# Five keep-busy products fewer, and the first maxima, a value's copy and the weight pieces moved, in the prologue of a gated cross-attention block

## The chip, the cores and the metric

One core of one Trainium2 chip runs the whole kernel. The metric is the time of one execution on the device in microseconds (us). The engines are PE (TensorE), DVE (VectorE), ACT (ScalarE), POOL (GpSimd) and SP (SyncE, which here issues DMAs and nothing else). Each runs its own stream of instructions in order, and they wait for each other by semaphores.

## The reference

The block takes x (4 x 512 x 512) and a context (4 x 1024 x 512), all float32. It has 16 heads of 32 columns.

```python
def qdq(x):                      # int8 fake quantisation along the last axis
    s = max(max(abs(x)) / 127, 1e-8)
    return clip(round(x / s), -127, 127) * s

def xattn(x, cond):
    q = qdq(x) @ qdq(wq).T + bq
    k, v = split(cond @ wkv.T + bkv)
    o = softmax(q k.T / sqrt(32)) @ v          # per head
    return qdq(o) @ qdq(wp).T + bp

def ffn(x):                      # gate_w, up_w, down_w rounded to float8_e4m3
    return ((silu(x @ gate_w * gate_scale) * (x @ up_w * up_scale)) @ down_w) * down_scale

x = x + tanh(g_xattn) * xattn(layernorm(x), ctx)
x = x + tanh(g_ffn) * ffn(layernorm(x))
```

## The kernel before

The four batches are computed one after the other. For each, a first stage makes q, k and v, a second the scores, exponentials and weighted sums in 32 units (4 groups of 4 heads by 8 tiles of 128 keys), and a third the projection and the feed-forward part. For batches 1 to 3 the first stage lies inside the stages of the batch before. For batch 0 it is a prologue of some 70 us, and only the prologue and the 32 units behind it are touched by the change.

**Products in two halves.** Keys and values are made from float16 pairs: a high part and a low part (what the high part left). A tile of keys (`K0` to `K7`) or values (`V0` to `V7`) takes 12 products of 128 x 512 into one bank of PSUM. The bias of a value tile is a 13th product, of ones with `bv_rows`, that POOL prepares (lines 735 to 743, semaphore `bv_set`). The 8 x 512 columns of values are copied out by ACT (line 909, semaphore `v_out`), the highs of q and k are made by ACT (lines 843, 850), the lows by DVE (`q_low` line 1178, `k_low` line 1165).

**The order on PE in the prologue** (lines 1777 to 1842): the keys; 12 products whose result nobody reads (line 1796); the turn of the quantised wq (line 1536), behind DVE's clip of it (line 1271); the first 8 of the 13 products of V0 and V1 (line 1570); the turn of quantised x (line 1536, behind ACT's line 876); its scales (line 1593); the four q tiles (line 1552, behind ACT's copies, line 880); the last 5 products of V0 and of V1 (lines 1576, 1577, behind `bv_set`); then V2 to V7 (line 1552); then the scores of the first unit (line 1716). `A_BANK` gives each result its bank. V0, V2 and V6 share bank 1; V1, V3 and V7 share bank 2, so that V2 waits until ACT has copied V0, and V3 until it has copied V1.

**The steps of the maxima.** The shift that each softmax needs is a maximum over keys. It is made in steps, laid into the products by tables. A step D (`difference`) is two products of q with half the difference of two halves of the keys (line 1621), which ACT turns into a doubled Relu (line 896, semaphore `diff_kept`). A step R is two products of q with the second half of the keys into banks 6 and 7 (line 1688), which DVE adds to the Relu and reduces to a maximum (line 1211, two instructions and a read of the accumulator each). PE's next R waits for DVE's reduction of the one before (`m_free`). A step S turns a finished group's maxima on PE (line 1643), and DVE clips them into `crow` (line 1198). `rest(n)` is the pair R of step n and D of step n+1. `STEPS0` says behind which tile's half each pair goes: before, `Q3` carries D0, `V2` to `V5` two pairs each (R0 to R7), `V6` S of group 0 and R8, `V7` R9; the rest goes to the units (`UNIT_STEPS0`).

**The weight pieces.** The gate, up and down weights arrive as 36 pieces of 256 KB and are rounded to float8 on the way. For each piece SP loads it (line 564), DVE makes its magnitude in two instructions (`w_magnitudes`, lines 1301 and 1304), and POOL rounds it in two (`round_weights`, lines 722 and 724, semaphore `w_done`). There are four buffers: pieces 0 to 3 are loaded early, and the load of piece k waits until piece k-4 is rounded. Before, DVE makes one magnitude behind each of V2 to V7.

**SP's queue.** SP issues in the order in which its program is written:

```python
stack(kst, (khi, khi, klo), 1)
load_weights(W_AHEAD["shift0"])     # up to piece 7: waits for w_done of pieces 1, 2, 3
shift_row(0, 0)                     # crow of group 0 into row 96 of qst
```

`shift_row` is line 588. The first scores of unit 0 (line 1716) contract 97 rows, of which row 96 is this one, and wait for the DMA to land (`stack_in[0]`).

Of the kernel before, what the change touches and what calls it, by code (L numbers as in the profile page):

```python
# [22 lines left out]
CT, NT, MT, FT = C // P, N // P, M // P, F // P  # L23
# [28 lines left out]
BEGUN = 2  # L52
# [20 lines left out]
def rest(n):  # L73

    return [("R",) + DIFFS[n][1:]] + DIFFS[n + 1:n + 2]


STEPS0 = {"Q3": [DIFFS[:1]], "V2": [rest(0), rest(1)], "V3": [rest(2), rest(3)], "V4": [rest(4), rest(5)],
          "V5": [rest(6), rest(7)], "V6": [[("S", 0, 0)], rest(8)], "V7": [rest(9), []]}
_first = 10  # L80

UNIT_STEPS0 = {u: rest(_first + u) if _first + u < len(DIFFS) else [] for u in range(G * MT)}
# [136 lines left out]
def a_count(name):  # L219
    return A_SEQ0.index(name) + 1  # L220


def by_act(name):

    return name[0] == "V"
# [117 lines left out]
def build(nc, ctxT, x, wq, wkvT, wp, gate_w, up_w, down_w, bqT, bkT, bv, bp, gsT, usT, ds,  # L343
          g_x, g_f, out):
    with ExitStack() as ctx:
# [135 lines left out]
        def bank(n, rows=P, dt=F32):  # L481
            v = ps[0:rows, n, :]
            return v if dt == F32 else v.bitcast(dt)
# [330 lines left out]
        def _(act):  # L814
# [72 lines left out]
            def differences(b, steps):  # L887

                for s in steps:
                    if s[0] != "D":  # L890
                        continue
                    n, first_bank = DIFFS.index(s), diff_bank(b, s)
                    act.wait_ge(diff_full, diff_count(b, s))
                    if n >= 2:
                        act.wait_ge(m_free, FREE_AFTER[b, ("R",) + DIFFS[n - 2][1:]])
                    nc.scalar.activation(kept(b, n), ps[:, first_bank:first_bank + 2, :], ACT.Relu,  # L896
                                         scale=2.0).then_inc(diff_kept, 1)

            for c in range(CT):
                if c == CT - 1:  # L900
                    for part in STEPS0[f"Q{c}"]:
                        differences(0, part)
                q_half(0, c)
            for name in A_SEQ0[-MT:]:
                for part in STEPS0.get(name, []):
                    differences(0, part)
                if by_act(name):
                    act.wait_ge(a_full, a_count(name))
                    nc.scalar.copy(vv[:, int(name[1:]), :], bank(A_BANK[name])).then_inc(v_out, 1)  # L909
            def projection_weights(u):  # L910

                if u in WP_ROWS:
# [122 lines left out]
        def _(dve):  # L1035
# [150 lines left out]
            def maxima(b, steps):  # L1186

                for s in steps:
                    kind, g, i = s
                    if kind in "WD":  # L1190
                        continue
                    if kind == "K":
                        if b == 0 or g > 0:
                            key_difference(b, g)
                        continue
                    if kind == "S" and b == 0:
                        dve.wait_ge(m_full, FULL_AT[b, s])
                        nc.vector.tensor_scalar(crow_rows(g), bank(PAIR, HG), CMAX, -CMAX, ALU.min,
                                                ALU.max).then_inc(crow_ready, 1)
                        continue  # L1200
                    if kind == "S":
                        dve.wait_ge(d_full, d_full_count(b - 1, f"TOP{g}"))
                        nc.vector.tensor_scalar(crow_rows(g), bank(d_bank(b - 1, f"TOP{g}"), HG), CMAX, -CMAX, ALU.min,
                                                ALU.max).then_inc(d_free, 1)
                        continue
                    n = g * PARTS + i
                    dve.wait_ge(m_full, FULL_AT[b, s])
                    dve.wait_ge(diff_kept, b * len(DIFFS) + n + 1)
                    for k in range(2):
                        j = 2 * (i % 2) + k  # L1210
                        ins = nc.vector.tensor_tensor_reduce(  # L1211
                            kept(b, n)[:, k, :], bank(PAIR + k), kept(b, n)[:, k, :], 1.0, -3.0e38, ALU.add,
                            ALU.max, mx[:, g % 2, i // 2, 0, j:j + 1])
                    ins.then_inc(m_free, 1)
# [109 lines left out]
            for n in range(CT):  # L1324
# [5 lines left out]
                    first_lows(K_SEQ0[7:])  # L1330
                if 1 <= n < CT - 1:
                    q_low(0, n - 1, a_free)
            for n in range(MT):
                if n == BEGUN + 1:
                    key_difference(0, 1)
                for k, part in enumerate(STEPS0.get(f"V{n}", [])):
                    maxima(0, part)
                    if n == BEGUN:
                        q_low(0, CT - 2 + k, a_free)
                if n >= MT - W_EARLY:  # L1340
                    w_magnitudes()

            for b in range(B):
# [187 lines left out]
        def _(pe):  # L1531
# [256 lines left out]
            for k, name in enumerate(K_SEQ0):  # L1788
# [3 lines left out]
                    pe.wait_ge(dve_setup, 3 * CT)  # L1792
                a_wait(name)
                k_product(bank(A_BANK[name]), int(name[1:]), a_full)
            for _ in range(CT * 3):
                nc.tensor.matmul(bank(6), wkv_hi[:, 0, 0:P], ctx_hi[:, 0, 0:512], start=True, stop=True)
            pe.wait_ge(pool_setup, 7)
            pe.wait_ge(wq_clipped, 1)
# [31 lines left out]
            pe.wait_ge(bv_set, 5)  # L1830
            for n in range(BEGUN):
                end_v(bank(A_BANK[f"V{n}"]), n, a_full, (ones[:, :], bv_rows[:, :]))
            for n in range(BEGUN, MT):
                first_v(n)
            pe.wait_ge(rows_set, 1 + G)
# [163 lines left out]
```

## Time and profile before

| | us |
|---|---|
| median of 3 runs | 893.6 (893.58 to 894.18) |
| profiled execution | 892.01, span 890.2 |
| PE busy | 855.0 (96%) |
| DVE busy | 674.1 (76%) |
| ACT busy | 563.1 (63%) |
| POOL busy | 256.3 (29%) |

The span runs from the first to the last instruction of the profiled execution; 1.8 us of that execution's time lie around it. Busy time is the sum of an engine's instructions with overlaps taken once. The granted clock of TensorE is 1.00 of full speed over the whole run by the profile's own account. Lines such as L1716 are lines of the kernel before.

### The profile page before, as it was taken

The numbers are of one execution on the slowest core, as the hardware profiler recorded it, in microseconds if no ns is written. First come the engines' busy times: TensorE is split into PE (matmuls) and PEld (weight loads), VectorE is DVE, ScalarE is ACT, GpSimd is POOL, SyncE is SP. The second block draws the span as 40 slices with busy tenths as digits, with TensorE's granted clock in tenths as the row PEclk, the third lists the DMA queues.
The fourth block names the chain that finished last, engine by engine and source line by source line (L and its number), as shares of the span: only waits on it lengthen the run. The fifth ranks groups of instructions, "written<-read, shape, count | busy, mean of one in ns | idle before, by whom it ended". The sixth has DMA issues, their size and how long they took to land.

```text
span 890.2 us, 14133 instructions
## 1 busy us (share of the span) xinstructions
PE 855.0 (96%) x5188; PEld 334.5 (38%) x5188; DVE 674.1 (76%) x1307; ACT 563.1 (63%) x771; POOL 256.3 (29%) x254
## 2 busy tenths in 40 slices
PE   7989999999899999899999999999999999999998
PEld 3432222354333322235433332225433322224984
DVE  5978967979766778878876768986967778779322
ACT  5758987752466569783555649885356779972440
POOL 1337767872257300020017700002002210011340
PEclk9999999999999999999999999999999999999999
DMA  9335334221111332200211143300010024200001
GB/s 322 124 92 151 89 112 112 83 83 44 47 46 39 101 108 60 48 1 1 48 30 48 38 120 91 76 5 1 15 39 1 1 52 113 57 1 25 14 1 48
DMA packets 37317, 55.32 MB, mean 62 GB/s; under 512 B 9024, under 2 KB 15488, under 8 KB 37248
## 3 DMA queue, kind: packets, MB, share of 16 engines
q1 hardware_dynamic: 35328, 48.13, 19.0%
q0 software_dynamic: 1920, 6.29, 2.4%
q8 instruction: 41, 0.67, 0.3%
q14 instruction: 28, 0.23, 0.1%
HBM read 31.21 MB, written 4.19 MB: 40 GB/s over the span
## 4 chain that ended last, share of the span: by engine, by line
PE 74%; DVE 11%; ACT 7%; issue 6%; DMA 0%; SPq 0%; ACTq 0%; DVEq 0%
PE ps L1552 37%; PE ps L1753 8%; PE ps L1716 8%; PE ps L1733 8%; ACT r L946 5%; PE ps L1688 4%; DVE acc L1236 4%; PE ps L1747 3%; PE ps L1536 2%; PE ps L1784 1%; PE ps L1761 1%; DVE kst L1211 1%; PE ps L1643 1%; DVE r L1211 0%; DVE q_reg L1178 0%
## 5 line engine op out<-in xcount | busy, mean ns | idle before, releaser
L946 ACT ACTIVATE r<-ps 128x1024 f32<-128x1024 f32 (+1 forms) x300 | 253.3, 902 | 54.2 <-PE ps L1716 51.7
L1211 DVE CUSTOM_DVE_ANT_0 kst<-ps,kst 128x512 f32<-128x512 f32 x192 | 124.5, 685 | 30.3 <-PE ps L1688 29.0
L1716 PE MATMUL ps<-qst,kst 97*128 97x512 f16 x512 | 137.1, 382 | 3.5 <-DVE acc L1316 1.8
L1733 PE MATMUL ps<-r,vv 128*32 128x512 f32 x1024 | 136.4, 604 | 3.4 <-ACT r L946 3.2
L1236 DVE TENSOR_TENSOR acc<-acc,r 128x1024 f32<-128x1024 f32 x120 | 138.7, 1216 | 0.0
L896 ACT ACTIVATE kst<-ps 128x1024 f32<-128x1024 f32 x96 | 98.1, 1022 | 54.2 <-PE ps L1621 53.9
L1552 PE MATMUL ps<-xs,w_up 128*128 128x512 f16 (+1 forms) x480 | 93.3, 337 | 0.0
L1552 PE MATMUL ps<-xs,w_gate 128*128 128x512 f16 (+1 forms) x480 | 93.2, 337 | 0.0
L1716 PEld LDWEIGHTS ps<-qst,kst 97*128 97x128 f16 x512 | 40.4, 97 | 139.3 <-ACT r L946 89.4
L1021 ACT ACTIVATE qst<-ps,gs_c 128x512 f32<-128x512 f32 (+1 forms) x60 | 36.1, 601 | 67.1 <-PE ps L1552 67.1
L1496 DVE SCALAR_TENSOR_TENSOR xq<-ps,us_c,qst 128x512 f32<-128x512 f32 (+1 forms) x60 | 38.6, 643 | 45.5 <-PE ps L1552 45.5
L1552 PEld LDWEIGHTS ps<-xs,w_gate 128*128 128x128 f16 x480 | 45.1, 98 | 36.2 <-issue 5.2
L1552 PEld LDWEIGHTS ps<-xs,w_up 128*128 128x128 f16 x480 | 44.0, 98 | 35.8 <-issue 8.2
L1688 PE MATMUL ps<-k_reg,q_reg 32*128 32x512 f16 x256 | 49.6, 385 | 3.7 <-DVE mx L1211 3.0
L1621 PE MATMUL ps<-acc,q_reg 32*128 32x512 f16 x256 | 49.6, 384 | 3.1 <-issue 3.1
L750 POOL TENSOR_TENSOR xres<-xres,bp_bc 128x512 f32<-128x512 f32 x12 | 14.9, 1268 | 129.6 <-ACT r L954 129.1
L711 POOL TENSOR_TENSOR rstd<-mv,mhalf 128x4 f32<-128x4 f32 (+1 forms) x9 | 10.3, 1145 | 144.4 <-DVE mv L1098 127.5
L1236 DVE TENSOR_TENSOR acc<-r 128x1024 f32<-128x1024 f32 x24 | 28.3, 1221 | 28.9 <-ACT r L946 28.9
L1552 PE MATMUL ps<-wkv_hi,ctx_hi 128*128 128x512 f16 x120 | 45.6, 380 | 1.1 <-ACT vv L909 1.1
L1747 PE MATMUL ps<-r,esel 128*32 128x512 f32 x352 | 46.4, 599 | 0.0
L1552 PE MATMUL ps<-wkv_hi,ctx_lo 128*128 128x512 f16 x120 | 45.5, 379 | 0.0
L1552 PE MATMUL ps<-wkv_lo,ctx_hi 128*128 128x512 f16 x120 | 45.5, 379 | 0.0
(204 smaller groups left out, 1399.0 us busy)
## 6 DMA issues: line engine op xcount, KB each, us to landing
kst<-k_reg SPq DMA_DIRECT2D x192, 64.0 KB
qst<-q_reg SPq DMA_DIRECT2D x192, 32.0 KB
xs<-in_x SPq DMA_DIRECT2D x4, 1024.0 KB, 6.9
cf<-in_ctxT POOLq DMA_DIRECT2D x16, 256.0 KB, 3.4
xres<-in_x SPq DMA_DIRECT2D x3, 1024.0 KB, 5.2
out<-xres SPq DMA_DIRECT2D x12, 256.0 KB, 2.0
acc<-in_down_w SPq DMA_DIRECT2D x10, 256.0 KB, 2.7
acc<-in_ctxT POOLq DMA_DIRECT2D x8, 256.0 KB, 3.3
```

What stands on the lines that cost most here:

```text
L896: nc.scalar.activation(kept(b, n), ps[:, first_bank:first_bank + 2, :], ACT.Relu, scale=2.0).then_inc(diff_kept, 1)
L946: nc.scalar.activation(prob[:, s:s + heads, :], ps[:, first_bank:first_bank + heads, :], ACT.Exp, scale=SCALE).then_inc(exp_done, 1)
L1211: ins = nc.vector.tensor_tensor_reduce(kept(b, n)[:, k, :], bank(PAIR + k), kept(b, n)[:, k, :], 1.0, -3.0e38, ALU.add, ALU.max, mx[:, g % ...
L1236: nc.vector.tensor_tensor(sums, other, prob[:, p:p + ADD_HEADS, :], ALU.add).then_inc(p_dve, 1)
L1496: nc.vector.scalar_tensor_tensor(out=fus[:, i % 2, width], in0=bank(d_bank(b, name))[:, width], scalar=us_c[:, tile:tile + 1], in1=tmp[:, ...
L1552: mm = nc.tensor.matmul(out, l, r, start=(k == 0), stop=(k == len(terms) - 1))
L1621: mm = nc.tensor.matmul(bank(first_bank + k), qhi[rows, g, i // 2 * P:(i // 2 + 1) * P], kdiff[rows, g % 2, :], start=True, stop=True)
L1688: mm = nc.tensor.matmul(bank(PAIR + k), qhi[rows, g, t * P:(t + 1) * P], khi[rows, g, 512:1024], start=True, stop=True)
L1716: mm = nc.tensor.matmul(bank(first_bank + k), kst[0:97, g % 2, j + k, t * P:(t + 1) * P], qst[0:97, g % 2, j + k, :], start=True, stop=True)
L1733: mm = nc.tensor.matmul(ps[j * DH:(j + 1) * DH, O_BANK, :], vv[:, t, h * DH:(h + 1) * DH], prob[:, p_slot(b, u, j), :], start=(t == 0), st ...
L1747: mm = nc.tensor.matmul(ps[j * DH:(j + 1) * DH, DEN_BANK, :], esel[:, g, :], prob[:, p_slot(b, u, j), :], start=(u == (MT - 1 if b else 0) ...
L1753: mm = nc.tensor.matmul(out[:, cols], f2_at(b, part, i)[:, t * P:(t + 1) * P], w_down[:, i, cols], start=(i == 0 and part == 0), stop=(i = ...
```

## The change

The change rewrites parts of the prologue of batch 0.

- PE issues 7 products at line 1796 where there were 12.
- The steps of the maxima begin one tile earlier: R0 and D1 go between the end of V1 and V2; V2, V3 and V4 carry the pairs of R1 to R6; V5 carries R7 alone. V6 (S, R8) and V7 (R9) and all units stay as they are.
- ACT does the Relu of D0 ahead of the third query half where it was ahead of the fourth, and copies V0 ahead of the fourth where it was behind it.
- DVE makes the low part of Q2 ahead of R0, that of Q3 and the key difference of group 1 behind R0 and ahead of R1. (Before, these stood behind R0, behind R1 and ahead of R2.)
- DVE makes no weight magnitude behind V2, one each behind V3 to V6, and two behind V7.

SP's program and POOL's are not touched.

```diff
--- before.py
+++ after.py
@@ -75,8 +75,8 @@
     return [("R",) + DIFFS[n][1:]] + DIFFS[n + 1:n + 2]
 
 
-STEPS0 = {"Q3": [DIFFS[:1]], "V2": [rest(0), rest(1)], "V3": [rest(2), rest(3)], "V4": [rest(4), rest(5)],
-          "V5": [rest(6), rest(7)], "V6": [[("S", 0, 0)], rest(8)], "V7": [rest(9), []]}
+STEPS0 = {"Q3": [DIFFS[:1]], "V1": [rest(0)], "V2": [rest(1), rest(2)], "V3": [rest(3), rest(4)],
+          "V4": [rest(5), rest(6)], "V5": [rest(7), []], "V6": [[("S", 0, 0)], rest(8)], "V7": [rest(9), []]}
 _first = 10
 
 UNIT_STEPS0 = {u: rest(_first + u) if _first + u < len(DIFFS) else [] for u in range(G * MT)}
@@ -896,17 +896,21 @@
                     nc.scalar.activation(kept(b, n), ps[:, first_bank:first_bank + 2, :], ACT.Relu,
                                          scale=2.0).then_inc(diff_kept, 1)
 
+            def first_values(name):
+                act.wait_ge(a_full, a_count(name))
+                nc.scalar.copy(vv[:, int(name[1:]), :], bank(A_BANK[name])).then_inc(v_out, 1)
+
             for c in range(CT):
+                if c == 2:
+                    for part in STEPS0[f"Q{CT - 1}"]:
+                        differences(0, part)
                 if c == CT - 1:
-                    for part in STEPS0[f"Q{c}"]:
-                        differences(0, part)
+                    first_values("V0")
                 q_half(0, c)
-            for name in A_SEQ0[-MT:]:
+            for name in A_SEQ0[-MT + 1:]:
                 for part in STEPS0.get(name, []):
                     differences(0, part)
-                if by_act(name):
-                    act.wait_ge(a_full, a_count(name))
-                    nc.scalar.copy(vv[:, int(name[1:]), :], bank(A_BANK[name])).then_inc(v_out, 1)
+                first_values(name)
             def projection_weights(u):
 
                 if u in WP_ROWS:
@@ -1330,14 +1334,14 @@
                     first_lows(K_SEQ0[7:])
                 if 1 <= n < CT - 1:
                     q_low(0, n - 1, a_free)
-            for n in range(MT):
-                if n == BEGUN + 1:
+            q_low(0, CT - 2, a_free)
+            for n in range(1, MT):
+                for part in STEPS0[f"V{n}"]:
+                    maxima(0, part)
+                if n == 1:
+                    q_low(0, CT - 1, a_free)
                     key_difference(0, 1)
-                for k, part in enumerate(STEPS0.get(f"V{n}", [])):
-                    maxima(0, part)
-                    if n == BEGUN:
-                        q_low(0, CT - 2 + k, a_free)
-                if n >= MT - W_EARLY:
+                for _ in range((0, 0, 0, 1, 1, 1, 1, 2)[n]):
                     w_magnitudes()
 
             for b in range(B):
@@ -1792,7 +1796,7 @@
                     pe.wait_ge(dve_setup, 3 * CT)
                 a_wait(name)
                 k_product(bank(A_BANK[name]), int(name[1:]), a_full)
-            for _ in range(CT * 3):
+            for _ in range(7):
                 nc.tensor.matmul(bank(6), wkv_hi[:, 0, 0:P], ctx_hi[:, 0, 0:512], start=True, stop=True)
             pe.wait_ge(pool_setup, 7)
             pe.wait_ge(wq_clipped, 1)
@@ -1830,6 +1834,9 @@
             pe.wait_ge(bv_set, 5)
             for n in range(BEGUN):
                 end_v(bank(A_BANK[f"V{n}"]), n, a_full, (ones[:, :], bv_rows[:, :]))
+                for part in STEPS0.get(f"V{n}", []):
+                    for s in part:
+                        maxima(0, s)
             for n in range(BEGUN, MT):
                 first_v(n)
             pe.wait_ge(rows_set, 1 + G)
```

## Rows read from the trace of the kernel before

**Rows 1.** Page, part 4: shares of the chain that ended last, by engine.
```profile
PE 74%; DVE 11%; ACT 7%; issue 6%; DMA 0%; SPq 0%; ACTq 0%; DVEq 0%
```

**Rows 2.** Timeline of PE, 28 to 49 us: start us, length us, what, [idle before <-releaser].
```profile
28.59 2.75 PE L1796 MATMUL ps<-ctx_hi,wkv_hi 128*128 128x512 f16 x12
31.18 1.06 PE L1536 MATMUL ps<-identb,w_down 128*128 128x128 bf16 x16
...
36.34 1.07 PE L1536 MATMUL ps<-identb,xq 128*128 128x128 bf16 x16 [0.65 <-ACT xq L876]
...
42.99 1.04 PE L1576 MATMUL ps<-wkv_lo,ctx_hi 128*128 128x512 f16 x4
...
45.25 0.39 PE L1577 MATMUL ps<-r 33*128 33x512 f16 x1
46.70 0.39 PE L1552 MATMUL ps<-wkv_hi,ctx_hi 128*128 128x512 f16 x1 [1.07 <-ACT vv L909]
...
48.11 0.39 PE L1688 MATMUL ps<-k_reg,q_reg 32*128 32x512 f16 x2
```

**Rows 3.** Timeline of PE, 54 to 71 us.
```profile
54.95 0.39 PE L1688 MATMUL ps<-k_reg,q_reg 32*128 32x512 f16 x2 [1.20 <-DVE mx L1211]
...
59.44 0.39 PE L1552 MATMUL ps<-wkv_hi,ctx_hi 128*128 128x512 f16 x1
...
63.38 0.39 PE L1552 MATMUL ps<-wkv_hi,ctx_hi 128*128 128x512 f16 x1
...
67.16 0.39 PE L1552 MATMUL ps<-wkv_hi,ctx_hi 128*128 128x512 f16 x1
...
70.61 0.60 PE L1716 MATMUL ps<-qst,kst 97*128 97x512 f16 x2
```

**Rows 4.** Timeline of DVE, 29 to 79 us.
```profile
29.48 0.68 DVE L1271 TENSOR_SCALAR w_down<-w_down 128x2048 bf16<-128x2048 bf16 x1
...
48.53 0.69 DVE L1211 CUSTOM_DVE_ANT_0 r<-ps,r 128x512 f32<-128x512 f32 x1 [3.19 <-PE ps L1688]
...
49.76 0.74 DVE L1178 SCALAR_TENSOR_TENSOR q_reg<-r,bq_c,q_reg 128x512 f16<-128x512 f32 x1
...
52.97 0.68 DVE L1183 CUSTOM_DVE_ANT_0 acc<-k_reg 128x512 f16<-128x512 f16 x1
...
68.63 0.29 DVE L1304 TENSOR_SCALAR acc<-acc 128x512 bf16<-128x512 bf16 x1
...
78.02 1.35 DVE L1183 CUSTOM_DVE_ANT_0 acc<-k_reg 128x512 f16<-128x512 f16 x1
```

**Rows 5.** Timeline of ACT, behind its copy of V7.
```profile
71.30 3.29 ACT L946 ACTIVATE r<-ps 128x512 f32<-128x512 f32 x6
```

**Rows 6.** Timeline of POOL, 41 to 72 us.
```profile
41.22 1.15 POOL L743 TENSOR_TENSOR r<-bv_bc,r 1x512 f16<-1x512 f32 x1
...
66.36 1.16 POOL L724 TENSOR_TENSOR w_gate<-xres 128x512 f16<-128x512 f32 x1
...
70.24 1.41 POOL L724 TENSOR_TENSOR w_gate<-acc 128x512 f16<-128x512 f32 x1
```

**Rows 7.** Timeline of SP's DMA issues, from 67 us.
```profile
67.54 0.33 SPq L564 DMA_DIRECT2D xres<-in_gate_w  x1
67.91 0.71 SPq L588 DMA_DIRECT2D qst<-crow  x1
```

**Rows 8.** Timeline of SP's DMA issues, around 774 us.
```profile
773.88 0.63 SPq L588 DMA_DIRECT2D qst<-crow  x1
```

**Rows 9.** Timeline of PE's weight loads, around 776 us.
```profile
775.88 0.55 PEld L1716 LDWEIGHTS ps<-qst,kst 97*128 97x128 f16 x4 [0.84 <-DMA qst<-crow]
```

**Rows 10.** Timeline of PE, its first products.
```profile
5.62 1.89 PE L1784 MATMUL ps<-ctx_hi,wkv_hi 128*128 128x512 f16 x4 [5.62 <-ACT ctx_hi L822]
...
10.46 1.03 PE L1784 MATMUL ps<-ctx_hi,wkv_hi 128*128 128x512 f16 x4
```

**Rows 11.** Timeline of PE, its longest idle time after the start.
```profile
226.76 0.39 PE L1621 MATMUL ps<-acc,q_reg 32*128 32x512 f16 x2 [2.59 <-issue]
```

## The prediction

> **What bounds the kernel now.** I read the chain of waits first: 74% of it is PE and 11% DVE [rows 1], so a change in the prologue counts only as far as it moves the moment at which PE gets on to the units. Next I read the timeline of PE from 28 us to the first scores, looking for places where it stands still. Three of them matter: 0.65 us before the turn of x (waiting for ACT's xq), 1.07 us before V2 (waiting for ACT's copy of V0) [rows 2], and 1.20 us before the pair R3 in V3 (waiting for DVE) [rows 3]. Besides, 12 products in 2.6 us (28.59 to 31.18) do nothing but keep PE busy [rows 2]. The first scores begin at 70.61, right behind V7 [rows 3]. Then I read the timelines of DVE, ACT, POOL and SP over the same stretch [rows 4 to 7], because every moved step has a follower there. SP's are the rows to look at: the shift row for unit 0 is issued at 67.91 only, right behind the load of weight piece 7 at 67.54 [rows 7], and that load had waited for POOL's fourth round, which ends at 66.36 + 1.16 = 67.52 [rows 6]. So the first scores hang on two things, V7 and the fourth round, and before the change V7 is the later one by little.
>
> **Five products fewer.** One takes 2.59/12 = 0.216 us [rows 2], so PE gets through at 28.59 + 7 x 0.216 = 30.10. DVE's clip of wq ends at 29.48 + 0.68 = 30.16 [rows 4]; with 0.04 for the semaphore PE turns wq at 30.20 where it was 31.18: **0.98 earlier**, all but 0.1 of the 1.08 taken out. ACT copies the turned wq as soon as PE has it and makes xq next, and the turn of x waited for that xq [rows 2], so the 0.98 goes on through the turn, the q tiles and D0. Behind D0 stand the ends of V0 and V1, that were begun at 42.99 [rows 2], would be at 42.01, and need POOL's bias rows. POOL ends those at 41.22 + 1.15 = 42.37 [rows 6] whatever PE does, so they begin at 42.42: of the 0.98, **0.57** is left.
>
> **The first step behind V1, V0 copied earlier.** V1's bias product started at 45.25 and held PE for 0.32 [rows 2]; now R0 and D1 start at 45.57 - 0.57 = 45.00, and V2 at 45.32 where it was 46.70. ACT's copy of V0 costs nothing there: V0 is full 1.3 to 1.4 behind 42.42, one ACT instruction on such a tile takes 0.55 (six in 3.29 [rows 5]), and PE needs the bank at 45.32 only. The price of R0's place is on DVE. It starts R0 0.43 after PE (48.11 to 48.53), is through it in 1.23 (48.53 to 49.76), and has the low part of Q3 (0.67 to the next start) and the key difference (0.61) next [rows 2, 4], so R1 begins at 45.43 + 1.23 + 0.67 + 0.61 = 47.94 and has released PE 1.31 later, at 49.25. PE wants R2 at 48.5 and gets it at 49.3, **a new wait of 0.8** in V2. V3 then starts at 49.3 + 0.32 + 0.32 = 49.96. The wait of 1.20 in V3 [rows 3] goes, since both additions are behind DVE.
>
> **V3 to V7.** V4 started at 54.95 + 0.32 + 0.32 = 55.59. A tile with two pairs takes 59.44 - 55.59 = 3.85, one with S and R8 67.16 - 63.38 = 3.78, one with one pair 70.61 - 67.16 = 3.45 [rows 3]. V3 and V4 take 3.85 each (V5 starts at 57.66), V5 is now of the last kind (V6 at 61.11), V6 as before (V7 at 64.89), V7 as before: PE wants the first scores at 68.34. That is **2.27 earlier** than 70.61, and it is what the change would bring if nothing else were late. The same S, Rs and Ds are done, so DVE, ACT and PE have no more work than before.
>
> **The weight pieces, and what is late next.** Before, the fourth magnitude stood behind R7, in V5; now it stands behind R8, in V6, where the fifth was. The fifth ended at 68.63 + 0.29 = 68.92 [rows 4], and POOL's round of it at 70.24 + 1.41 = 71.65 [rows 6], 2.73 later. With V6 and V7 2.27 earlier, and R9 and the next magnitude behind it on DVE just as they stood before, POOL's fourth round ends at 71.65 - 2.27 = **69.38, where it was 67.52**. SP waits for it with the load of piece 7, and the shift row is queued behind that load: issue at 69.38 + (67.91 - 67.52) = 69.77. SP's issues in front of that load I cost at nothing: they wait for rounds one to three, the last of which is a whole tile (3.8) ahead of the fourth; were that cover gone, the 12 copies of keys ahead of piece 5 would be the next thing late.
>
> What the row needs from issue to landing the stretch doesn't show. From below: at 773.88 such a row is issued, and PE's load, for which it was the last thing to come, starts at 775.88, 2.00 later [rows 8, 9]. From above: 67.91 to 70.61 is 2.70, and PE did not wait [rows 3, 7]. I take 2.3, nearer to the end that is a measured wait, with something for the 256 KB load just in front. The first scores start at 69.77 + 2.3 = 72.07, **3.7 later than PE wants them** and 1.46 later than before. But before, they were 0.3 too early for ACT: its first exponential started at 71.30, 0.69 behind the scores [rows 5], for the copy of V7 came first. Now ACT is idle and starts 0.44 behind them (0.39 for the product, 0.05 for the semaphore): 72.51, which is **1.2 later** than 71.30. With the bounds of the landing, 0.9 to 1.6.
>
> POOL's rows leave one choice. L724 took 1.41 in the fifth round and 1.16 in the fourth [rows 6], the longer one with DVE's magnitude beside it. As the new fourth round has the fifth's neighbours, I took the longer. The Trainium skill's page "SBUF — State Buffer", section "Who interferes with whom", has it that DVE and POOL share a pair of ports and that the first to issue holds it for its whole instruction. By that rule, were POOL first, its round would be 0.25 shorter and the sum 0.95.
>
> Behind the first exponential I find nothing that takes up the delay: unit 0 is the same chain of scores, exponentials and R10 as before, R9 and both magnitudes behind it are over on DVE before R10 comes, and the pieces that are loaded behind the shift row are first used two units later. Time **+1.2**: the profiled execution's 892.01 would become 893.2, the median of 893.6, which is 1.6 above it, 894.8. A measurement of this kernel tells 0.2%, some 1.8 us, from no change, so this is within it.
>
> **Rivals.**
> A, the scores do not wait for the shift row, and all of the 2.27 arrives: 893.6 - 2.3 = 891.3. For it: before the change no wait for this row shows anywhere near 70 us, and ACT's V7 copy moves along with PE. Against it: SP's written order and the two rows at 67.5 and 67.9, one behind the other and behind POOL. 8%.
> B, the clock. Four products take 1.89 at the start, 0.43 apart, which is the 1.2 GHz level; from about 10.46 four take 1.03, 0.216 apart, the 2.4 GHz level [rows 10]. Before that start PE had been idle. The longest idle time since is 2.59, and the product behind it takes 0.39, as the same kind does at 48.11 [rows 2, 11]; the new wait is longer, some 3.3. If the clock falls in it and comes back as slowly as at the start, 4.8 us are run at half pace, which costs up to 2.4: +3.6, 897.2, slower. It decides only if it falls at all. 7%. The Trainium skill's page "TensorE: Matmul & The Clock Gate", Part 1, says that an idle window brings the half rate.
> C, slower too, in V2 on DVE: the key difference takes 1.35 beside POOL's work at 78.02 where it took 0.68 at 52.97 [rows 4], and if PE comes to V0's end no earlier than 42.99, the 0.57 is lost as well. All of V3 to V7, the fourth round and the shift row are later by what is added there, up to 1.2: +2.4, 896.0. It decides from 0.6 on. Against it: POOL has nothing to do between its bias rows and the first magnitude. 16%.
>
> **How the numbers follow.** The sum has 69%, spread over +0.2 to +2.0, with 3 of it past 1.8. Slower by over 0.2%: 3 + 7 + 16 = 26%. Faster: A's 8%. Within: 66%. The range runs from 892.6, below the sum's lowest bound with the scatter of the medians, to 896.4, so that it takes in C and leaves out A and most of B.
>
> **What would show it.** Right: 7 products at L1796 and a turn at 30.2; no wait before V2, one of about 0.8 in V2, none in V3; V7 at 64.9; POOL's fourth round ending near 69.4; the shift row issued near 69.8; PE idle for about 3.3 with the crow DMA as the releaser, first scores near 72.1. Wrong: first scores at 68.3 (A), products of 512 columns 0.43 apart behind the wait (B), V7 later than 65.4 (C), or units that close up the 1.2.

## The result, and the profile after

The changed kernel takes 896.4 us (median of 7 executions, 893.78 to 896.97) where the kernel before, measured with it, takes 893.58 (7 executions, 890.72 to 894.36). The ratio is 1.0039 with a 95% interval of 1.0026 to 1.0051: **slower by 0.4%, some 3.5 us by the ratio, 2.8 by the medians**. That is on the edge of the range (892.6 to 896.4), past the forecast of "within 0.2%", and well past the 894.8. Three executions below were disturbed, far from all others of their kernel (978.8 us and more), and are left out of all counts.

The timeline of PE in the changed kernel's prologue; columns as in rows 2. Lines have moved by 4: L1720 here is the scores' L1716, L1692 is R's L1688.

```profile
27.67 1.67 PE L1800 MATMUL ps<-ctx_hi,wkv_hi 128*128 128x512 f16 x7
29.47 1.05 PE L1540 MATMUL ps<-identb,w_down 128*128 128x128 bf16 x16
...
34.62 1.07 PE L1540 MATMUL ps<-identb,xq 128*128 128x128 bf16 x16 [0.65 <-ACT xq L876]
...
41.68 1.02 PE L1580 MATMUL ps<-wkv_lo,ctx_hi 128*128 128x512 f16 x4 [0.34 <-POOL r L743]
...
44.24 0.39 PE L1692 MATMUL ps<-k_reg,q_reg 32*128 32x512 f16 x2
...
46.25 0.39 PE L1692 MATMUL ps<-k_reg,q_reg 32*128 32x512 f16 x2 [0.22 <-DVE mx L1215]
...
48.75 0.39 PE L1692 MATMUL ps<-k_reg,q_reg 32*128 32x512 f16 x2 [0.70 <-DVE mx L1215]
...
65.72 0.39 PE L1692 MATMUL ps<-k_reg,q_reg 32*128 32x512 f16 x2
...
71.63 0.59 PE L1720 MATMUL ps<-qst,kst 97*128 97x512 f16 x2 [3.80 <-DMA qst<-crow]
```

This execution runs ahead of the one before by 0.92 from the start (keys done at 27.67, not 28.59 [rows 2]), so 0.9 is to be added to compare. Of the three old waits, the 0.65 before the turn of x is as it was, and the ones before V2 and in V3 are gone. New and smaller are 0.34 at the end of V0, and 0.22 and 0.70 in V2. But the first scores come at 71.63 + 0.9 = 72.5 where they came at 70.61 [rows 3], behind a new wait of 3.80 whose releaser is the shift row's DMA. POOL and SP of the same kernel, same columns, show what the row was queued behind:

```profile
67.39 1.42 POOL L724 TENSOR_TENSOR w_gate<-xres 128x512 f16<-128x512 f32 x1
```

```profile
66.10 3.06 SPq L564 DMA_DIRECT2D xres<-in_gate_w  x2
69.21 0.71 SPq L588 DMA_DIRECT2D qst<-crow  x1
```

POOL's fourth round ends at 68.81, the second load of the first SP line (piece 7) goes out behind it, then the row at 69.21; it lands 2.4 later.

The second half of the loss is in the view of busy time by stretches of the changed kernel (columns: stretch, its length, busy time of each engine with its instructions, granted clock, DMA share, GB/s):

```profile
68.00:72.00 4.00, 0.37 (x2) 0.13 (x2) 2.41 (x3) 0.56 (x2) 3.69 (x4) 1.00 0.53 144
72.60:79.40 6.80, 6.71 (x26) 1.06 (x26) 3.13 (x8) 4.70 (x9) 3.76 (x5) 0.50 0.94 259
79.40:90.00 10.60, 10.60 (x80) 2.41 (x76) 9.51 (x24) 8.66 (x15) 6.02 (x6) 1.00 0.28 78
226.00:229.60 3.60, 1.00 (x6) 0.22 (x3) 3.53 (x8) 0.00 (x0) 2.36 (x2) 1.00 0.19 47
229.60:233.00 3.40, 3.40 (x11) 1.19 (x10) 0.25 (x1) 1.64 (x2) 2.86 (x3) 0.50 0.27 62
```

The granted clock, third from the end of each line, is 0.50, the 1.2 GHz level, for 6.8 us behind the new wait, and again for 3.4 near 230, behind the wait of 2.6 that both kernels have there [rows 11]. In the profiled execution before, the same stretches were at 1.00:

```profile
70.60:78.00 7.40, 6.53 (x43) 1.40 (x42) 5.51 (x13) 6.55 (x13) 5.72 (x6) 1.00 0.85 244
...
226.80:231.00 4.20, 4.20 (x23) 1.66 (x24) 2.06 (x5) 2.46 (x3) 3.13 (x3) 1.00 0.27 62
```

The two profiled spans, 894.4 and 890.2, differ by 4.2. At the first scores the difference is 1.02, when PE resumes near 229 it is 2.52 (229.28 against 226.76 [rows 11]), and behind the second low stretch it is 4.18 (a wait of PE for DVE that ends at 362.63 against 358.45) and stays there. So 1.5 were lost in and behind the first low stretch, 1.66 in the second. That the second belongs to the change is not shown: the wait of 2.6 in front of it stands in both kernels. Of the ten profiled executions here with this wait, seven have a stretch at 0.50 behind it: six of the seven with the change's order of steps, one of the three with the order before.

**Reading the time by mean clock.** Every execution's record has its mean granted clock. A stretch of 3.4 us at 0.50 takes 1.7 of some 890 us off, 0.002 of the mean, so the mean tells how much time was spent at half the clock: in the traces, 0.998 goes with 3.4 us of it, 0.996 with 6.8, 0.994 with 10.2 and 0.992 with 13.7. The kernel before stands in several such classes, and its own median of 893.6 is a mixture. Over the 80 executions that the comparisons below made of it:

| mean clock | kernel before: executions, median | changed kernel (16, two runs) |
|---|---|---|
| 1.000 | 33, 891.5 | 0 |
| 0.998 | 16, 893.4 | 0 |
| 0.996 | 25, 893.8 | 3, 894.2 |
| 0.994 | 4, 895.9 | 11, 896.4 |
| 0.992 and under | 2, 896.3 | 2, 897.0 and 899.0 |

In the classes 0.996 and 0.994 the two kernels are within 0.5 of each other. That doesn't make the late row free, since the stretches needn't lie at the same places and needn't cost the same there. The changed kernel spent 6.8 us or more at half the clock in all of its 16 executions, the kernel before in 31 of 80 (and some time in 47).

### The profile page after: what moved, and what is told of

The parts are those of the page before. It is cut to its first block, busy times and chain, and to the rows that moved or that the text cites. A ratio compares the mean times of both kernels' runs of the same rounds, so it can differ in the third digit from the quotient of the medians.

```text
span 894.4 us, 14123 instructions
## 1 busy us (share of the span) xinstructions
PE 857.5 (96%) x5183; PEld 334.2 (37%) x5183; DVE 675.5 (76%) x1307; ACT 563.7 (63%) x771; POOL 256.5 (29%) x254
## 4 chain that ended last, share of the span: by engine, by line
PE 70%; DVE 15%; issue 9%; ACT 4%; DMA 1%; SPq 0%; POOL 0%; ACTq 0%; DVEq 0%
PE ps L1556 35%; PE ps L1757 8%; PE ps L1720 8%; PE ps L1737 7%; DVE acc L1240 5%; PE ps L1692 4%; PE ps L1751 4%; ACT r L950 2%; PE ps L1540 2%; PE ps L1765 1%; DMA r<-in_ctxT 1%; DVE kst L1215 1%; DVE q_reg L1182 1%; PE ps L1647 1%; DVE r L1386 1%
## 5 line engine op out<-in xcount | busy, mean ns | idle before, releaser
L1720 PE MATMUL ps<-qst,kst 97*128 97x512 f16 x512 | 138.1, 385 | 6.9 <-DMA qst<-crow 3.8
L1720 PEld LDWEIGHTS ps<-qst,kst 97*128 97x128 f16 x512 | 40.5, 97 | 143.7 <-ACT r L950 87.6
L1692 PE MATMUL ps<-k_reg,q_reg 32*128 32x512 f16 x256 | 49.8, 386 | 3.3 <-DVE mx L1215 2.7
```

Source lines behind the costliest of these rows:

```text
L1692: mm = nc.tensor.matmul(bank(PAIR + k), qhi[rows, g, t * P:(t + 1) * P], khi[rows, g, 512:1024], start=True, stop=True)
L1720: mm = nc.tensor.matmul(bank(first_bank + k), kst[0:97, g % 2, j + k, t * P:(t + 1) * P], qst[0:97, g % 2, j + k, :], start=True, stop=True)
```

## The experiments

Theory 1: the moved magnitudes make the shift row late, and the clock falls in or behind the wait for it. The rivals: something else holds the first scores; the five products or chance bring the low clock. For an edit that was measured at several clocks, "at 1.000" gives its median over the executions with a mean clock of 1.000.

### The shift row ahead of piece 7

```diff
-W_AHEAD = {"keys1": 5, "shift0": 8, ...
+W_AHEAD = {"keys1": 5, "shift0": 7, ...
```

> The changed kernel with one number different: SP issues the shift row ahead of the load of weight piece 7, so the row waits for POOL's third round and no longer for the fourth. Theory 1 (the wait of 3.8 us before the first scores is the row queued behind that load, and the low clock follows from the wait): the row is issued some 2 to 4 us earlier, PE's idle time before the first scores goes or falls under 0.5 us, all rows up to 100 us have the granted clock 1.00, and the time is 891 to 892, 2.3 below the kernel before. Theory 2 (the row isn't what the scores wait for, another landing of the same semaphore is: the copies of q and k): the wait stays within 0.5 us of 3.8, time 896. Theory 3 (the wait costs nothing of its own, the clock falls for lack of the five products): the wait goes but the clock is still 0.5 somewhere from 30 to 80 us, and the time stays above 893.5.

Measured 893.55 (12 executions), ratio to the kernel before 1.0002 (0.9987 to 1.0017). SP's timeline and PE's first scores:

```profile
58.90 7.48 SPq L578 DMA_DIRECT2D kst<-k_reg  x12
66.42 0.58 SPq L564 DMA_DIRECT2D acc<-in_gate_w  x1
67.04 0.46 SPq L564 DMA_DIRECT2D xres<-in_gate_w  x1
67.55 0.71 SPq L588 DMA_DIRECT2D qst<-crow  x1
```

```profile
70.39 0.59 PE L1720 MATMUL ps<-qst,kst 97*128 97x512 f16 x2 [1.63 <-DMA qst<-crow]
```

The releaser is the row, so theory 2 of this run falls. But it is a miss for my numbers (891 to 892, and the upper level up to 100 us): 1.63 of the wait stays, and the granted clock was 0.51 from 73.1 to 76.5 in this trace. None of the 12 executions is at 1.000; the 5 at 0.998 have a median of 890.9, the 7 below it stand between 893.1 and 896.1. A low stretch behind a shortened wait is also what theory 3 (the five products) would give; the kernel with 12 products and late magnitudes, below, excludes it. The row is now behind SP's own queue: the 12 copies of keys stand behind the load of piece 4, which waits for POOL's first round, itself one tile later than before. The prediction had named these copies as the next thing late and set their cost at nothing.

### PE kept busy in the wait

```diff
             pe.wait_ge(minus_in, 16)
+            pe.wait_ge(v_out, v_out_count("V5"))
+            for _ in range(16):
+                nc.tensor.matmul(bank(3), wkv_hi[:, 0, 0:P], ctx_hi[:, 0, 0:512], start=True, stop=True)
```

> The changed kernel with 16 products of 512 columns (3.5 us) whose result nobody reads, into a free bank, between V7 and the first scores. The wait for the shift row stays, PE is busy in it. Theory 1: the first scores start when they did (71.6 in the changed kernel's trace, give or take 0.3), the granted clock stays 1.00 from 28 to 100 us, and what the first low stretch cost comes back, 1.5 to 2.4: time 894.3 to 895, about 1.2 above the kernel before. Theory 2 (the low clock costs little because DVE bounds the first units anyhow): time within 0.5 of 896.4. If the products themselves delay the scores, the first scores start later than 71.9.

Measured 894.54 (12 executions), ratio 1.0017 (1.0005 to 1.0029), 1.9 below the changed kernel's 896.4. At 1.000 (4 executions, a class that the changed kernel never reached) it is 893.0, 1.5 above the kernel before. Its PE timeline, and the stretch behind it by busy time:

```profile
68.02 3.63 PE L1846 MATMUL ps<-ctx_hi,wkv_hi 128*128 128x512 f16 x16
71.78 0.60 PE L1720 MATMUL ps<-qst,kst 97*128 97x512 f16 x2
```

```profile
72.00:80.00 8.00, 7.39 (x48) 1.63 (x50) 5.42 (x13) 7.05 (x13) 5.24 (x5) 1.00 0.75 228
```

The wait is as long as before, with the 16 products in it, and the clock stays up. This divides the loss: **1.5 is the late row itself, 1.9 is the clock behind the wait**. Class by class the 1.5 is 1.3 to 1.5: 893.0 against 891.5 at 1.000, 894.7 against 893.4 at 0.998, 895.3 against 893.8 at 0.996. The only low stretch left in this trace is 3.4 us from 226.9 on. The run also shows that PE wanted the scores at 68.02.

### The magnitudes as before

```diff
-                for _ in range((0, 0, 0, 1, 1, 1, 1, 2)[n]):
+                for _ in range((0, 0, 1, 1, 1, 1, 1, 1)[n]):
```

> The changed kernel with the weight magnitudes where they were before the change: one behind each of V2 to V7. Theory 1: the fourth magnitude stands behind R7 again, POOL's fourth round ends near 64, the shift row is issued near 64.5 and has landed before V7 ends, so no wait before the first scores and no low clock up to 100 us: 891 to 892. Rival (the magnitude behind V2 delays R3 on DVE, which is why it was moved): V7 ends 0.5 to 1 later than in the changed kernel, time 892 to 893.

Measured 891.09 (10 executions), ratio 0.9973 (0.9959 to 0.9987); at 1.000 889.55. SP and PE:

```profile
62.22 2.32 SPq L564 DMA_DIRECT2D xres<-in_gate_w  x2
64.58 0.71 SPq L588 DMA_DIRECT2D qst<-crow  x1
```

```profile
67.74 0.61 PE L1720 MATMUL ps<-qst,kst 97*128 97x512 f16 x2
```

One number put back, and the row goes out at 64.58 and the wait is gone. R3 is not late for the magnitude behind V2. All the rest of the change, taken together, is worth 1.9 to 2.5 of a gain; the moved magnitudes turn it into a loss. Yet there was a low stretch here too, with no wait over 0.8 in the 10 us in front of it:

```profile
60.00:70.80 10.80, 9.93 (x51) 3.52 (x49) 7.56 (x18) 6.02 (x11) 8.07 (x8) 1.00 0.71 213
70.90:74.30 3.40, 3.40 (x15) 0.53 (x18) 2.54 (x8) 2.56 (x5) 2.11 (x3) 0.50 0.65 179
```

My "no low clock up to 100 us" was wrong, then. With the wait of 3.8 every execution measured has a low clock; without it a low stretch can still come.

### The magnitudes moved in the kernel before

```diff
-                if n >= MT - W_EARLY:
-                    w_magnitudes()
+                for _ in range((0, 0, 0, 1, 1, 1, 1, 2)[n]):
+                    w_magnitudes()
```

> The kernel before with the magnitudes alone moved (none behind V2, two behind V7), all else as before. Theory 1: POOL's fourth round ends near 71.6 where it ended at 67.5, the row is issued near 72.0, the first scores start near 74.3 (3.7 later than before), the clock is 0.5 for some microseconds behind the wait: time 3.4 plus 1.5 to 2.4 above the kernel before, 898 to 899.5, with DVE's wait before R3 shortened by the missing magnitude (0.8 at most to take off). Rival (the placement of the magnitudes is worth little by itself): within 1 us of the kernel before.

Measured 898.14 (6 executions), ratio 1.0050 (1.0033 to 1.0066), as forecast, and the rival falls:

```profile
73.79 0.59 PE L1716 MATMUL ps<-qst,kst 97*128 97x512 f16 x2 [3.84 <-DMA qst<-crow]
```

The same wait, 3.84, from this part alone, with the same 6.8 us at half the clock behind it. None of the 6 executions is above 0.996. This kernel has its 12 products, so the low clock doesn't come from the five that are missing.

### The copies and the row ahead of pieces 4 to 7

```diff
-W_AHEAD = {"keys1": 5, "shift0": 8, ...
+W_AHEAD = {"keys1": 4, "shift0": 4, ...
```

> The changed kernel with SP's order alone different: the 12 copies of keys and the shift row are issued ahead of the loads of pieces 4 to 7. The moved magnitudes stay as the change has them. With the first experiment SP issued the row at 67.55 and PE still waited 1.63, because the 12 copies (7.5 us) stood behind the load of piece 4; here they no longer do. Theory 1: the row is issued as soon as DVE has clipped it (near 64), no wait before the first scores, and the time is that of the kernel with the magnitudes as before: executions at a mean clock of 1.000 at 889.5, median 891. Rival (late magnitudes cost in the units too, where DVE is the bound up to 94 us): 0.5 to 1 above that, or DVE waits for a piece not yet loaded behind V7.

Measured 893.85 (12 executions), ratio 1.0007 (0.9996 to 1.0018); at 1.000 892.4, 0.9 above the kernel before and 2.9 above the kernel with the magnitudes as before (889.5). The rival's second half came true (DVE waits for a piece), and its price is far over the 0.5 to 1 that I gave the first half. PE gets its row (first scores at 68.12, no wait), and pays later, on DVE, shown with PE behind it:

```profile
71.33 0.43 DVE L1305 TENSOR_SCALAR acc<-acc 128x512 uint16<-128x512 uint16 x1 [3.52 <-DMA acc<-in_gate_w]
71.79 0.29 DVE L1308 TENSOR_SCALAR acc<-acc 128x512 bf16<-128x512 bf16 x1
72.01 0.43 DVE L1305 TENSOR_SCALAR acc<-acc 128x512 uint16<-128x512 uint16 x1
72.47 1.14 DVE L1308 TENSOR_SCALAR acc<-acc 128x512 bf16<-128x512 bf16 x1
73.53 0.68 DVE L1215 CUSTOM_DVE_ANT_0 r<-ps,r 128x512 f32<-128x512 f32 x1
```

```profile
74.88 0.39 PE L1692 MATMUL ps<-k_reg,q_reg 32*128 32x512 f16 x2 [0.94 <-DVE mx L1215]
```

The fifth magnitude has to wait for piece 4, two magnitudes then stand in front of R10, and R11 waits for that. Neither of the two orders tried on SP gives what the early magnitudes give.

### Twelve products again

The line of the magnitudes as before the change, and:

```diff
-            for _ in range(7):
+            for _ in range(CT * 3):
```

> The changed kernel with the magnitudes as before the change and 12 keep-busy products again. By the steps of the prediction the five products are worth 0.98 at the turn of wq and 0.57 behind POOL's bias rows: V7 and the first scores 0.5 to 0.6 later than with 7, executions at a mean clock of 1.000 at 890.1 where they are 889.3 to 889.9 with 7. Rival (the five products kept the clock up): fewer executions with a mean clock under 1.000 than with 7.

Measured 891.37 (12 executions), ratio 0.9982 (0.9971 to 0.9992); at 1.000 890.0, 0.4 above the kernel with 7 (3 executions each, which overlap: 889.12 to 890.48 and 889.31 to 889.94). Of the 12, 9 have a mean clock under 1.000; with 7 it was 7 of 10. So the five products did not hold the clock up, and they cost at most a few tenths.

### Seven products alone

```diff
-            for _ in range(CT * 3):
+            for _ in range(7):
```

(in the kernel before)

> The kernel before with 7 keep-busy products and nothing else. The turn of wq comes 0.98 earlier. Here V2 waits for ACT's copy of V0, which stands behind the fourth query half, so not POOL's bias rows but the query path sets V2, and all of the 0.98 should reach the first scores, as long as the shift row (landed at about 70.1 in the trace of before, as it is bound to POOL's fourth round, which moves along) lets it: 0.6 to 1.0 faster than the kernel before, at equal mean clock (891.4 before at 1.000). Rival: nothing arrives, since POOL or the row is fixed: within 0.2.

Measured 893.77 (12 executions), ratio 1.0007 (0.9992 to 1.0021); at 1.000 (2 executions) 891.2, 0.3 below. A miss: I expected 0.6 to 1.0. Its keys are done at 27.99 and V2 starts at 45.98, 17.99 apart; before, it was 46.70 - 28.59 = 18.11 [rows 2]. So 0.12 arrived (0.19 if counted from the end of POOL's bias rows). V2 still waits for ACT's copy of V0:

```profile
45.98 0.39 PE L1552 MATMUL ps<-wkv_hi,ctx_hi 128*128 128x512 f16 x1 [1.37 <-ACT vv L909]
```

That copy stands behind ACT's fourth query half, which DVE scales (L1171), and V2 starts 2.11 behind the start of that scaling in both kernels: 43.87 and 45.98 here, 44.59 and 46.70 before. The timelines of DVE and POOL tell why the scaling is no earlier:

```profile
38.85 1.54 DVE L1171 SCALAR_TENSOR_TENSOR r<-ps,sw_q,r 128x512 f32<-128x512 f32 x2 [0.56 <-PE ps L1552]
40.31 0.74 DVE L1165 SCALAR_TENSOR_TENSOR k_reg<-ps,bk_c,k_reg 128x512 f16<-128x512 f32 x1
40.97 1.42 DVE L1178 SCALAR_TENSOR_TENSOR q_reg<-r,bq_c,q_reg 128x512 f16<-128x512 f32 x1
```

```profile
40.69 1.15 POOL L743 TENSOR_TENSOR r<-bv_bc,r 1x512 f16<-1x512 f32 x1
```

The low part of Q0 (L1178) takes 1.42 where it takes 0.74 elsewhere (49.76 [rows 4]), and it ends some 0.6 behind POOL's last bias row. Before, it came after the bias rows were done. Arriving earlier, DVE runs into POOL's instruction and loses 0.68, nearly all that it had gained by then. That fits what the Trainium skill's page "SBUF — State Buffer", section "Who interferes with whom", says: a DVE instruction with two inputs in SBUF contends with a GpSimd instruction that reads SBUF. This one has two, `r` and the high part of q.

### Busy products in front of batch 1's first D step

The line of the magnitudes as before the change, and, at the head of `difference`:

```diff
+                if b == 1 and n == 0:
+                    pe.wait_ge(d_free, d_free_count(0, "X2T0"))
+                    for _ in range(11):
+                        nc.tensor.matmul(bank(6), wkv_hi[:, 0, 0:P], ctx_hi[:, 0, 0:512], start=True, stop=True)
```

> The changed kernel with the magnitudes as before the change, and 11 products whose result nobody reads in the wait of 2.6 us in front of the first D step of batch 1 (near 222 us), which all kernels have. Theory on the clock: the second low stretch, near 226 to 230, is brought by this wait and by where it falls in time, so it goes, while the one near 71 stays by chance. Executions at a mean clock of 0.998 become 1.000 or stay at 0.998 with the stretch near 71; the median comes down by 0.5 to 1.5 to near 890, and the fastest stay at 889.3. Rival (the low clock comes at random or from the light load alone, not from the wait): the granted clock is still 0.5 near 226 in most executions and the median stays at 891.

Measured 890.15 (median of 6 executions), ratio 0.9970 (0.9958 to 0.9983), against 891.09 and a ratio of 0.9973 with the magnitudes alone. Of the 6, 3 are at 1.000 (889.4), against 3 of 10. The trace is of an execution of 3836 us, so where the low stretches lay can't be read from it, and the counts are too small to settle it. Inconclusive by itself.

### The changed kernel again

No edit.

> The changed kernel as it is, on the chip of the next run, for more executions by mean clock. Theory: no execution has a mean clock of 1.000, since the wait of 3.8 us brings a low stretch every time; at 0.996 its time is within 0.5 of the kernel before at 0.996 (893.8), at 0.994 within 1 of it (895.9), and the median is 2 to 3.5 above the kernel before because more of its executions stand in the low classes. Rival: some executions at 1.000, near 893, so that the wait alone doesn't bring the low clock.

Measured 896.35 (9 executions), ratio 1.0045 (1.0030 to 1.0060). None at 1.000 or 0.998, as expected, and the class 0.994 (7 executions, 896.35) is within 0.5 of the kernel before's 895.9. Two misses: the one execution at 0.996 took 895.16, 1.4 above 893.8, and the median is 4.4 above that of the kernel before (891.95 here, where 8 of its 14 executions were at 1.000), over the 2 to 3.5 expected. The trace has the wait again (3.88, behind the row) and again 0.50 for 6.8 us behind it and for 3.4 near 230.

### The key difference ahead of the late magnitudes

The line of the magnitudes as before the change, and, for the next batch's keys on DVE:

```diff
                     for n in range(8):
-                        if n == 1:
-                            key_difference(b + 1, 0)
                         beside(f"K{n}")
                         k_low(b + 1, n, d_bank(b, f"K{n}"), d_free)
+                        if n == 0:
+                            key_difference(b + 1, 0)
                         late_magnitudes(2 * (n == 0))
```

> The changed kernel with the magnitudes as before the change, and with the key difference of each next batch made by DVE right behind the low part of K0, ahead of two late magnitudes (before: behind them). The wait of 2.6 us in front of the first D step of batch 1 then ends about 2.1 earlier. Theory: 1.5 to 2.2 faster than with the magnitudes alone at equal mean clock (1.000: 887.4 to 888), and fewer executions with a low stretch near 226, median 888.5 to 889.5. Rival (DVE or POOL's late rounds bound that stretch): the wait moves behind D0 and less than 0.7 arrives.

Measured **887.79** (6 executions, 887.41 to 888.45), ratio 0.9943 (0.9927 to 0.9959): this kernel beats both. PE's wait at that place:

```profile
222.55 0.39 PE L1625 MATMUL ps<-acc,q_reg 32*128 32x512 f16 x2 [0.44 <-issue]
```

0.44 where there was 2.59 [rows 11]. It is real work moved, not filler; 4 of 6 executions are at 1.000 (887.8, where the magnitudes alone gave 889.55) and none is under 0.998.

### The same in the kernel before

The edit of `difference_first` in the kernel before, with nothing of the change.

> The kernel before with the key difference ahead of the late magnitudes and nothing of the change. It separates this edit from the change. Theory: at a mean clock of 1.000 1.8 below the kernel before (891.6), so 889.8, and the rest of the 3.8 of the combined kernel (1.9) belongs to the change with its magnitudes put back. The share of executions with a low stretch stays between that of the kernel before and that of the combined one. Rival (the gains overlap): more than 2.5 or less than 1 arrives.

Measured 889.34 (5 executions), ratio 0.9961 (0.9947 to 0.9974), all 5 at 1.000, 2.2 below the kernel before at 1.000. So the two gains add: 2.2 here, 1.6 more from the change with its magnitudes put back. All 5 stand at 1.000, where the kernel before, measured beside them, has 4 of 11 (33 of 80 in all). That ties a good part of its low stretches to the wait of 2.6.

### POOL's bias rows earlier

POOL's bias-row instructions (lines 733 to 745; they are five, not seven) moved ahead of the low parts of the value weights, in the kernel of `difference_first`.

> The kernel of the run before (magnitudes as before the change, key difference first) with POOL's seven bias-row instructions ahead of its four low parts of the value weights, in the time in which it waited for DVE. Theory: in the changed kernel the 0.98 of the five products shrank because those bias rows, done at 42.4 in the frame of before, hold V0's end, and because they keep DVE's low part of Q0 at 1.42 where it is 0.74 alone. With them early the end of V0 follows D0 at once, the low part of Q0 takes 0.74, and the first scores come 0.4 to 0.6 earlier: 887.2 to 887.5 at a mean clock of 1.000, where it was 887.4 to 887.8. Rival (the low parts of the value weights, now later on POOL, slow DVE's q path in the same way): no more than 0.1 of a gain, and low parts of Q0 still over 1.2.

Measured 888.73 (6 executions), ratio 0.9956 (0.9942 to 0.9970): slower than without by 0.9 by the medians, though the intervals of the two ratios overlap. The 0.4 to 0.6 of a gain did not come. Half of the theory holds. The low part of Q0 takes 0.74, and V0's end has no wait. But:

```profile
31.01 1.05 PE L1540 MATMUL ps<-identb,w_down 128*128 128x128 bf16 x16 [1.74 <-DVE w_down L1275]
```

DVE's clip of wq is now what PE waits for, 1.74, so that the gain is spent before it is made. In front of the clip DVE normalises x, four instructions from 24.24 on, and POOL's bias rows, which ran from 23.13 to 26.57, lie beside the first two:

```profile
25.48 2.29 DVE L1105 TENSOR_SCALAR xs<-xs,mv,rstd 128x512 f32<-128x512 f32 x3
```

```profile
25.35 1.22 POOL L738 TENSOR_TENSOR r<-bv_bc,r 1x512 f16<-1x512 f32 x1
```

Those two took 1.31 and 1.37, the other two 0.53 each, and in the kernel without this edit all four took 0.54. So the four took 3.52 for 1.91. The 1.6 lost there are most of the wait of 1.74, and they come with the bias rows' new place.

## Why the prediction was wrong

**Right: the mechanism of the first half, term by term.** The turn of wq came 1.80 behind the start of the 7 products (29.47 - 27.67; forecast 1.61; the clip ended 0.08 later against the keys than before, and the turn followed it by 0.15 where 0.04 was taken). V0's end waited for POOL's bias rows and began at 41.68 + 0.9 = 42.6 (forecast 42.42). The wait before V2 went, the one in V2 was 0.70 (forecast 0.8), with one of 0.22 ahead of it that the sum did not have, and the one in V3 went. PE wanted the scores at 68.0 by the run with busy products, whose keys are done at 27.92, so 0.7 ahead: 68.7 against 68.34. POOL's fourth round, with 1.42 for L724 where 1.41 was taken, ended at 68.81 + 0.9 = 69.7 (forecast 69.38), the row was issued at 70.1 (69.77), landed in 2.4 (2.3), and the first scores started at 72.5 (72.07). All of that was 0.3 to 0.5 later than forecast, and the cost of the row by itself was 1.5 (forecast 1.2). With the clock held up behind the wait the kernel takes 894.5, the forecast 894.8.

**Wrong: the step on the clock, in the rivals.** The sum had no term for it, and B, "if the clock falls in it", had 7%. In both traces of the changed kernel it was 0.50 for 6.8 us right behind the wait, and none of the 16 executions has a mean above 0.996. So the step that failed is the cost of the new wait: the sum had its length, and put the slower products behind it at nothing. The argument for 7% was that a wait of 2.59 had been followed by the upper level [rows 11]. That was one execution; by the classes above, the kernel before has a low stretch in 47 of 80, and the trace that I had happened to be one without. The Trainium skill's page "TensorE: Matmul & The Clock Gate", Part 1, which I had cited beside the 7%, says that an idle window brings the half rate; the trace of the changed kernel agrees, with 0.50 from 72.6 to 79.4 behind 3.8 idle. B's own price was about right: 1.9 measured by the run that fills the wait, at most 2.4 forecast.

**Also wrong, and small: 0.57 for the five products.** Between the kernels with 12 and 7 it was 0.4, and alone 0.3 at 1.000 and 0.1 by the trace. In the changed kernel's trace V0's end came 42.99 - 42.6 = 0.4 earlier. The prediction saw POOL's bias rows holding the end of V0, and did not see them holding DVE's low part of Q0, 1.42 for 0.74 in this kernel too: DVE then came to R0 0.65 behind PE (44.89 against 44.24) where 0.43 was forecast, and the difference is the wait of 0.22 in V2.

**The rivals.** A (no wait for the row) is excluded by the releaser, and by the wait, which shrinks when the row goes out earlier. B happened, on top of the sum: 897.2 was its time, 896.4 was measured. C (V3 to V7 later by DVE's key difference) did not happen: V3 came with no wait in it, and V7 began at 64.31 + 0.9 = 65.2, under the 65.4 that would have been its sign.

**Open.** Why the clock falls in some executions with no long wait in front (70.9 to 74.3 in the kernel with the magnitudes as before), and why not in all behind the same wait of 2.6, the runs don't settle. Nor do they say where the low stretches of the kernel before lie, since its one trace has none. Also open is how the 1.5 us behind the first low stretch divide between PE and the engines that wait for it.

## What to carry to other kernels

When a step is moved by one slot, follow it through every queue that it feeds, until something that PE waits for: here a magnitude on DVE, a rounding on POOL, a load on SP, and behind that load, in the same queue, a 4 KB row that had nothing to do with it. Price a new idle time of TensorE twice, once for its length and once for the clock behind it, and fill it or remove it; and before a single trace is taken as proof that the clock holds, look at the mean clock of many executions. Taking products out of a keep-busy loop gains only as far as nothing else holds the work behind it: of 0.98 at the loop, 0.4 was left at V0's end. And when work is moved into another engine's idle time, look at what a third engine does beside it (the bias rows beside DVE).

## What the hardware showed that I had not expected

- Equal times at half the clock don't cost the same: the kernel before is at 891.5 at a mean clock of 1.000, at 893.4 at 0.998, 893.8 at 0.996 and 895.9 at 0.994, steps of 1.9, 0.4 and 2.1. And a median moves with the mixture though no instruction does: 891.95 in one comparison of the kernel before, 893.57 in another.
- The granted clock was 0.50 for 6.8 us behind a wait of 3.80, and for 3.4 behind one of 2.60, in the same execution; in the kernel before, the same wait of 2.59 was followed by 1.00 in the profiled execution. Over ten profiled executions with this wait, seven had 0.50 behind it.
- In the kernel with the magnitudes as before, it was 0.50 for 3.4 us although PE had been busy 9.93 of the 10.8 us in front.
- DVE's low part of Q0 took 1.42 beside POOL's one-partition bias rows and 0.74 without them; two of its normalising instructions took 1.31 and 1.37 beside them, and 0.54 without.
